# The first layer's exponent extraction placed earlier in VectorE's order

## The reference, cut to what matters

```python
x = L0_attn_x                                    # (32, 512, 256) float32
x = x + _L0_attn_ref(_layernorm(x), w_q, w_k, w_v, w_out, softmax_scale)
x = x + _L0_ffn_ref(_layernorm(x), kernel, input_scale, kernel_scale, bias)
x = x + _L1_attn_ref(_layernorm(x), w_in, w_out)           # causal, alibi
x = x + _L1_ffn_ref(_layernorm(x), W, b, lora_down, lora_up, down_aux, up_aux)

def _L0_attn_ref(x, ...):       # one key head and one value head for 16 query heads
    q = (x @ w_q.T).reshape(B, S, 16, 16);  k = x @ w_k.T;  v = x @ w_v.T
    attn = softmax(einsum('bshd,btd->bhst', q, k) * softmax_scale)
    return einsum('bhst,btd->bshd', attn, v).reshape(B, S, D) @ w_out.T

def _L0_ffn_ref(x, kernel, ...):
    x_q = (x.astype(bfloat16).astype(float32) / s_in).astype(float8_e4m3fn)
    k_q = (kernel.astype(float32) / s_k).astype(float8_e4m3fn)
    return (x_q.astype(f32) @ k_q.astype(f32) * (s_in * s_k)).astype(bfloat16) + bias
```

## Time and profile before

| | |
|---|---|
| median of 3 runs | 3657.52 us (3643.35 to 3670.59) |
| the profiled execution's own time | 3658.99 us |
| its span, first to last instruction | 3657.2 us |
| mean granted TensorE clock | 0.974 |
| TensorE matmul busy | 3449.0 us, 94% of the span |
| VectorE busy | 2872.1 us, 79% |
| ScalarE busy | 2484.4 us, 68% |
| GpSimd busy | 2119.5 us, 58% |

### The profile page before, as it was taken

One profiled execution on the slowest core, in us unless ns is written; L12 is line 12 of the kernel. 1 busy time (PEld: TensorE's weight loads), 2 busy tenths in 40 slices (PEclk: granted clock), 3 DMA queues, 4 the chain that ended last, 5 costly groups with the idle time before them and its releaser, 6 DMA issues. The chain is left out here.

```text
span 3657.2 us, 79325 instructions
## 1 busy us (share of the span) xinstructions
PE 3449.0 (94%) x26824; PEld 1944.8 (53%) x26824; DVE 2872.1 (79%) x8451; ACT 2484.4 (68%) x5347; POOL 2119.5 (58%) x2340
## 2 busy tenths in 40 slices
PE   5999999999999999999689999999999999999997
PEld 2444444444444444444446666666666666666664
DVE  5899999999998999998267777677777777777773
ACT  2788888788788888887346666566666666666663
POOL 2377777677767777775745455455454554554542
PEclk7999999999999999999879999999999999999997
DMA  4344434433343444343466767767668668677761
GB/s 122 68 83 86 95 68 90 93 87 76 84 99 71 89 88 92 71 87 91 87 130 106 139 120 122 134 118 124 129 120 132 116 120 142 118 121 139 122 108 30
DMA packets 251934, 376.45 MB, mean 103 GB/s; under 512 B 21930, under 2 KB 122448, under 8 KB 251264
## 3 DMA queue, kind: packets, MB, share of 16 engines
q1 hardware_dynamic: 249484, 369.28, 53.2%
q10 hardware_dynamic: 2048, 2.10, 0.4%
HBM read 223.97 MB, written 136.95 MB: 99 GB/s over the span
## 5 line engine op out<-in xcount | busy, mean ns | idle before, releaser
L681 DVE TENSOR_REDUCE maxima<-ps_max 128x1 f32<-128x512 f32 x2048 | 1274.1, 680 | 98.2 <-PE ps_max L444 94.0
L1524 DVE CUSTOM_DVE_ANT_0 ps_max<-ps_max,mask 128x512 f32<-128x512 f32 (+3 forms) x2048 | 962.4, 515 | 353.4 <-PE ps_max L1246 350.7
L575 ACT ACTIVATE probs<-ps_rest 128x512 f32<-128x512 f32 x2048 | 1073.5, 602 | 226.7 <-PE ps_rest L457 224.1
L1397 ACT ACTIVATE probs<-ps_rest 128x512 f32<-128x512 f32 (+3 forms) x2048 | 773.4, 436 | 452.4 <-PE ps_rest L1267 400.0
L444 PE MATMUL ps_max<-k_op,q_op 48*128 48x512 f32 x2048 | 724.5, 446 | 61.8 <-DVE maxima L681 54.0
L457 PE MATMUL ps_rest<-q_op,k_op 50*128 50x512 f32 x2048 | 717.1, 441 | 0.3 <-ACT probs L575 0.2
L444 PEld LDWEIGHTS ps_max<-k_op,q_op 48*128 48x128 f32 x2048 | 340.2, 187 | 531.7 <-DVE maxima L681 411.5
L1246 PE MATMUL ps_max<-k_op,q_op 51*128 51x512 f32 (+3 forms) x2048 | 564.6, 366 | 23.8 <-DVE maxima L1524 4.0
L1267 PE MATMUL ps_rest<-q_op,k_op 53*128 53x512 f32 (+3 forms) x2048 | 559.6, 366 | 19.9 <-DMA q_op<-mrows 19.7
L478 PE MATMUL ps_pv<-probs,v_op 128*32 128x512 f32 x4096 | 543.0, 605 | 1.0 <-ACT oT L587 1.0
L1246 PEld LDWEIGHTS ps_max<-k_op,q_op 51*128 51x128 f32 x2048 | 315.4, 188 | 166.9 <-DVE maxima L1524 89.6
(11 more groups left out here) (145 smaller groups left out, 5465.3 us busy)
## 6 DMA issues: line engine op xcount, KB each, us to landing
qk_parts<-qparts SPq DMA_DIRECT2D x192, 512.0 KB, 3.2
q_op<-qk_parts SPq DMA_DIRECT2D x384, 256.0 KB, 7.8
k_op<-qk_parts SPq DMA_DIRECT2D x192, 256.0 KB, 10.5
xin<-in_x SPq DMA_DIRECT2D x32, 512.0 KB, 4.6
xres<-in_x SPq DMA_DIRECT2D x32, 512.0 KB, 4.8
x_mid<-xo SPq DMA_DIRECT2D x32, 512.0 KB, 3.2
xin<-x_mid SPq DMA_DIRECT2D x32, 512.0 KB, 7.1
xres<-x_mid SPq DMA_DIRECT2D x32, 512.0 KB, 15.8
```

The source lines that it names most:

```text
L575: act.activation(probs[:, quad % 2, at:at + S], ps_rest[:, bank("exp", b, p), :], ACT.Exp).then_inc(ps_out["exp"], 1)
L681: dve.tensor_reduce(at, ps_max[:, bank("max", c, k), :], AX.X, ALU.max).then_inc(ps_out["max"], 1)
L1397: act.activation(probs[quad % 2][:, at:at + nq], ps_rest[:, bank("exp", b, p), 0:nq], ACT.Exp).then_inc(ps_out["exp"], 1)
L1524: dve.tensor_tensor_reduce(row, row, mask[:, S - keys:S], 1.0, LOWEST, ALU.add, ALU.max, at).then_inc(ps_out["max"], 1)
```

## The change

One word of the first layer's plan moves. `exponent:0:-2` stood behind the pairs P23 and P24, and now stands behind the pairs P15 to P18, one line of the plan after `over:0:-2`. Only VectorE acts on this word. The instruction, its operands and its semaphores stay the same. On VectorE it now comes ahead of the maxima of P19 to P21, `split:2:0`, `otr:2:-1`, `otr:3:-1` and the maxima of P22 to P24, which it followed before. The orders of all other engines and the banks do not change.

```diff
 PPP m:1:0 stat2:2:-2 split_kv:0:1 V
 PPP load_m:1:0 stat2:3:-2 norm2:0:-2 V stat1:0:2 over:0:-2 cut_ont:0:-1 V
 PPP stat1:1:2
-V magic:0:-2 PPPP load_res:0:-1 fp8:0:-2 ont:0:-1
+V magic:0:-2 PPPP exponent:0:-2 load_res:0:-1 fp8:0:-2 ont:0:-1
 PPP split:2:0 load_q:0:1 otr:2:-1 V otr:3:-1
 P
-PP exponent:0:-2 m:2:0 V V cut_ont:1:-1 v:0:1 load_k:0:1 load_m:2:0
+PP m:2:0 V V cut_ont:1:-1 v:0:1 load_k:0:1 load_m:2:0
 PPPP V stat1:2:2
 PPP qk:1:1
```

## The result

The changed kernel is slower. The first comparison gave a median of 3717.09 us (3697.49 to 3739.9, 4 runs) against 3664.05, a ratio of 1.016 with a 95% interval of 1.008 to 1.023. A second one, with more runs on both sides, gave 3708.09 us against 3660.91, a ratio of **1.013** (1.0099 to 1.016): 47 us. The prediction said 3706, from 48 us on top of the time before, with a range of 3686 to 3721. The profiled execution of after took 3697.49 us, with a span of 3695.6.

The account below looks back on a forecast made before the run. TensorE was taken to set the pace, busy 51.27 of 53.00 us per batch. 30 x 1.60 = 48 us, with 0 for the change of layers, gave 3705.5 from the median 3657.52 and 3707.0 from the profile; forecast 3706, range 3686 to 3721.

Parts of the forecast that it names:

- The path to TensorE: Steady batches: P19 starts 1.72 us late, `otr:3` frees its bank late, so TensorE's `m:2` comes 1.60 us late.
- the wait alone: New place, each steady batch: VectorE waits 0.69 us for GpSimd to end `z8` before the exponent.
- The collision: New place: sharing a port with GpSimd's line 807, the exponent takes 1.11 us instead of 0.68.
- The slack of 0.12 us: Ahead of `m:2`: 0.08 us at the reciprocal of `otr:3` and 0.04 us before `m:2` absorb part of the delay.
- The duration of 1.11 us: Exponent at the new place, taken from its single earlier use directly behind `z8` with line 807 beginning alongside.
- The first rival: Burst P25 to P28: TensorE's 1.73 us idle per batch makes up the delay, giving 3658 us; chance 0.14.
- The second: New place: no collision with GpSimd, exponent 0.68 us, `m:2` 1.17 late, 35 us in all, 3694; chance 0.13.
- The clock: Steady batches: each pause brings on a lower granted clock, 1.4 us more per batch, 90 us in all, 3750; chance 0.04.
- Nobody takes this up. [...] I cost it at nothing: GpSimd's line 871 starts at about 1042.4 instead of 1045.53; the earlier rounding was costed at nothing.
- the 0 for the change of layers: Last uses of the exponent: VectorE's tile slip of about 4.6 us is covered by TensorE's waits; 0 taken.
- that of 13.88 us: Change of layers: TensorE's wait for the rounding stays, as the exponent at 1788.06 already started directly behind `z8`.
- VectorE's late tiles: Last use of the exponent: next tiles slip about 4.6 us, covered by TensorE's 5.67 us wait for the rounding.

Follow-up runs that it names:

- e3: Kernel before, with only a VectorE wait for `z8` added at the new place, exponent at its old place: 3696.28 us against 3660.91, ratio 1.0097.
- e8: Changed kernel with the statistics `stat2:3` three pairs sooner, so GpSimd ends `z8` sooner: 3691.30 us against 3662.05 before, 1 run.
- e9: Kernel before with only the statistics `stat2:3` three pairs sooner, exponent at its old place: 3680.06 us against 3666.38, 1 run.
- e4: Changed kernel with GpSimd's `cut_ont:0` (lines 807, 809) moved behind `magic`, away from the exponent: 3701.03 us against 3660.91 before, ratio 1.0091.
- e1: The changed kernel measured again, nothing else altered: 3708.09 us against 3660.91 before, ratio 1.013.
- e10: e7 measured again: 3658.75 us against 3666.38 before, ratio 0.9981.
- e7: Kernel before with the exponent at the new place only in the last three uses, at the change of layers: 3657.43 us against 3662.05, ratio 0.9976.

## Where the prediction was right, and the step that failed

**The path to TensorE** in the steady batches was right, in place and size. Each part has its own kernel, in us per batch more than before:

| | expected | measured |
|---|---|---|
| the wait alone (e3) | 0.57 | 0.60 |
| the exponent alone (e8 less e9) | 0.48 | 0.49 |
| both, no collision (e4) | 1.17 | 1.18 |
| all three, the changed kernel | 1.60 | 1.60 to 1.62 |

The collision is the difference of the last two rows, 0.43 us. The slack of 0.12 us ahead of `m:2` counts once: 0.69 + 0.60 - 0.12 = 1.17.

**The duration of 1.11 us**, taken from one single row with the same neighbours and not from the 30 with other ones, was right to 0.01 us. It was the largest open term, 0.43 us a batch.

**The first rival**, that TensorE makes up the delay, fell. VectorE's idle time ahead of P25 only grew. **The second**, no collision, fell with e1 and is what e4 had to be built for. **The clock**, which was to cost 1.4 us more in each batch, fell too: the distance is 1.60 to 1.62 us up and not 3.0, and the granted clock of the steady stretch rounds to 1.00.

**The step that failed** is "Nobody takes this up. [...] I cost it at nothing", of GpSimd's earlier rounding, and with it the 0 for the change of layers. It holds for the steady batches, which is all that the earlier trace rows could show. At the change of layers GpSimd's next work behind the rounding is the second layer's first norm, and TensorE waited 8.12 us for it. The row was among those I read the earlier trace rows, and I set it down as work of the second layer with no tie to the rounding. The chain on GpSimd, rounding, norm, line 1328, would have shown it.

The term was to be -5.8 us. From the last `m:2` to line 1328 the kernel before takes 1749.94 - 1731.40 = 18.54 us, the changed kernel 1792.48 - 1779.75 = 12.73, e1 12.80 and e10 12.83. Two things are in it. GpSimd's chain from the start of line 862 for c = 29 to line 1328 is 3.97 us shorter (1749.94 - 1726.46 = 23.48, then 1792.48 - 1772.97 = 19.51). And TensorE's own delay in this last batch, which the sum counted in full, is covered by the wait for that chain. Up to the last `m:2` TensorE is 48.35 us late, where the sum has 30 x 1.60 = 48. With the term it is 48 - 5.8 = 42.2 us, and the trace has 42.6 (e1: 40.0).

Of the two other waits there, that of 13.88 us was to stay and did not stay whole. TensorE now waits 6.17 us for `o_rows` ahead of it, and 5.96 us are left. The start of line 536 is 52.1 us behind line 1328, where it was 52.5, so nothing comes of it. VectorE's late tiles (3.28 us of waiting at 1874.62) come out of the old wait of 5.67, now 1.74, as forecast.

Against the first layer of the traces the forecast of 48 us is 5 to 8 us too high. The medians are up by 47 and 53 us, with 36 to 59 us in the second interval. That 48 lies so near to them is in part luck: the missing 5.8 us are made up by what comes behind the first layer, which none of these runs explains.

## What to carry to other kernels

When an instruction is moved forward on an in-order engine, ask two things: is its input ready at the new place, and which of the instructions that it overtakes has someone waiting without slack. Here a place three maxima sooner was free, and ahead of `otr:3` the same work cost 0.49 us a batch, or 1.6 us with the wait and the collision. For a duration, look for the row with the same neighbours on the engine that shares the port, even if it is only one. And an engine's earlier finish has to be followed through all stages, the seams between loops above all, before it is costed at nothing.

## What the runs showed of the hardware

The exponent (128 x 1024, 32 bits, in and out of SBUF) and the GpSimd instructions that it met (lines 807 and 809) did their work one after the other, whichever was first. The second one's wait stands in its own busy time: 0.68 became 1.10 or 1.35 us on VectorE, 0.62 became 0.90 and 1.28 became 1.59 on GpSimd. In these profiles the lock does not show as a wait, only as a longer instruction.

A pause of TensorE and a stretch at lower granted clock do not always fall together. Behind a wait of 3.60 us at the change of layers, e7 had 0.50 for 10 us and lost some 4 us by it (97.6 against 93.6 us to the last line 536); behind 1.44 us, e10 had 0.83. The kernel before, with the longest wait, 8.12 us, had 0.71 in the 10 us up to its end and 0.78 in the 10 us behind, so part of its low stretch fell into the wait.
